# Last layer of a four-layer graph kernel: for the units on the diagonal, VectorE raises the distances and GpSimd weights the edges in three steps

## The reference, cut to what matters

```python
deg = jnp.maximum(adj.sum(axis=1, keepdims=True), 1e-08)
w = adj / deg
log_ij = _logmap(x[:, None, :], x[None, :, :], 1.0)      # for every pair i, j
agg = jnp.einsum('ij,ijc->ic', w, log_ij)
out = _expmap(zeros, agg @ weight + bias, 1.0)           # then residual and layer norm
```

## Time and profile before

| what | us |
|---|---|
| median of three executions | 1662.96 |
| lowest, highest | 1653.44, 1667.85 |
| the profiled execution | 1664.92 |
| its span, first to last instruction | 1662.80 |
| last layer, first raise (L1442) to end of the last weighting (L674) | 1157.51 to 1608.20 |

### The profile page before, as it was taken

The page is one execution under the profiler, slowest core; times in us unless marked ns, Lnnn a source line. Parts: engine busy times, 40 slices in busy tenths (PEclk is TensorE's granted clock), DMA queues, the critical chain, the costliest instruction groups (busy, mean ns, idle before and its releaser), DMA issues.

```text
span 1662.8 us, 20844 instructions
## 1 busy us (share of the span) xinstructions
PE 1508.1 (91%) x7990; PEld 633.8 (38%) x7990; DVE 1175.8 (71%) x1579; ACT 946.1 (57%) x918; POOL 306.3 (18%) x154
## 2 busy tenths in 40 slices
PE   5999999989999699999999999988788889889870
PEld 1433333333333444444444444433333333333330
DVE  4677755557888655755857847477888787887867
ACT  1243388854343423323334346667889898998954
POOL 1000000000000000000000004594445343444430
PEclk9999999999999699999999999999999999999995
DMA  9999779968999334443443422246344454544500
GB/s 343 411 412 413 291 285 409 409 275 354 413 412 369 120 148 156 156 185 116 152 152 150 155 102 64 76 133 197 109 134 166 155 179 135 173 133 146 164 14 26
DMA packets 118107, 348.95 MB, mean 210 GB/s; under 512 B 6325, under 2 KB 31225, under 8 KB 117753
## 3 DMA queue, kind: packets, MB, share of 16 engines
q1 hardware_dynamic: 106784, 329.27, 52.9%
q10 hardware_dynamic: 11224, 18.36, 3.0%
HBM read 329.78 MB, written 17.83 MB: 209 GB/s over the span
## 4 chain that ended last, share of the span: by engine, by line
PE 62%; issue 15%; POOL 11%; DVE 6%; DMA 3%; ACT 2%; SPq 0%; POOLq 0%; ACTq 0%; DVEq 0%
PE ps L777 19%; PE ps L904 13%; POOL ring L674 11%; PE ps L910 10%; PE ps L715 4%; PE ps L716 3%; DMA ring<-in_adjT 3%; PE ps L933 2%; PE ps L849 2%; PE ps L741 1%; PE ps L939 1%; PE ps L731 1%; PE ps L797 1%; PE ps L851 1%; PE ps L853 1%
## 5 line engine op out<-in xcount | busy, mean ns | idle before, releaser
L1184 ACT ACTIVATE work<-ps,code_bias 128x1024 uint8<-128x1024 f32 x128 | 135.8, 1111 | 247.0 <-PE ps L716 238.7
L904 PE MATMUL ps<-ring,X 128*64 128x512 f32 x512 | 264.1, 597 | 13.3 <-DVE ring L1943 13.3
L905 PE MATMUL ps<-work,X 128*64 128x512 f32 x512 | 264.1, 598 | 0.0
L635 POOL TENSOR_SCALAR work<-ring 128x1024 int16<-128x1024 uint8 x24 | 69.4, 2898 | 1025.0 <-DMA ring<-codes 978.5
L1315 ACT ACTIVATE work<-ring 128x2048 f32<-128x2048 f32 x64 | 122.2, 1911 | 217.1 <-PE ps L912 196.1
L674 POOL TENSOR_TENSOR ring<-ring,work 128x1024 f32<-128x1024 f32 x80 | 190.0, 2375 | 253.1 <-DVE work L2199 252.9
L910 PE MATMUL ps<-work 128*64 128x512 bf16 x768 | 208.7, 381 | 0.0
L912 PE MATMUL ps<-work 128*64 128x512 bf16 x768 | 208.7, 381 | 0.0
L1006 PE MATMUL ps<-work 128*128 128x512 f32 x320 | 165.6, 642 | 0.0
L777 PE MATMUL ps<-ring,work 128*64 128x512 f32 x704 | 161.0, 599 | 1.1 <-DMA ring<-in_adjT 1.1
L1940 DVE TENSOR_SCALAR work<-ring 128x2048 bf16<-128x2048 f32 x64 | 78.5, 1226 | 107.3 <-PE ps L912 107.1
(11 more groups left out here) (332 smaller groups left out, 2642.5 us busy)
## 6 DMA issues: line engine op xcount, KB each, us to landing
ring<-in_adjT SPq DMA_DIRECT2D x90, 2048.0 KB, 11.5
work<-in_adjT SPq DMA_DIRECT2D x26, 2048.0 KB, 15.4
ring<-in_adjT SPq DMA_DIRECT2D x48, 1024.0 KB, 8.1
codes<-work ACTq DMA_DIRECT2D x64, 256.0 KB, 6.1
ring<-codes SPq DMA_DIRECT2D x32, 512.0 KB, 3.6
ring<-in_adjT SPq DMA_DIRECT2D x32, 512.0 KB, 3.5
X<-in_x ACTq DMA_DIRECT2D x1, 1024.0 KB, 6.8
work<-in_xT SPq DMA_DIRECT2D x2, 512.0 KB, 23.2
```

The costliest lines, as they stand in the source:

```text
L904: nc.tensor.matmul(ps[0:F, h, :], rows, ring[:, r, k, cols], start=start, stop=stop)
L905: nc.tensor.matmul(ps[F:P, h, :], rows, negs[:, pair, i, cols], start=start, stop=stop)
L1184: nc.scalar.activation(codes[:, u, k:k + 2, :].rearrange("p k c -> p (k c)"), ps[:, bank:bank + 2, :].rearrange("p k c -> p (k c)"), ACT.Relu,
```

## The change

Own units only. Their raise moves from ScalarE to VectorE, straight ahead of `multiply` there (a `tensor_scalar` with add and max from PSUM into `u.log`, and a wait of VectorE on its own semaphore before `multiply`). Their angle product on VectorE goes. GpSimd takes it over: edges x inverse root as soon as that exists, then the angle clipped in place, then edges x angle. `wait_for_log` gives the raise of unit n the right releaser of the log buffer of unit n-3: the angle product of an off unit or the first GpSimd step of an own one. `g_made` now counts off units alone.

```diff
--- before.py
+++ after.py
@@ -271,6 +271,14 @@
         def off_at(n):
             u = unit_at(n)
             return u if u and u.off else None
+
+        def wait_for_log(eng, u):
+
+            w = unit_at(u.n - 3)
+            if w and w.off:
+                eng.wait_ge(g_made, w.offs + 1)
+            if w and not w.off:
+                eng.wait_ge(edges_scaled, w.place + 1)
 
         PAIRS = 2 * NS
         L2_TILES = [(Q, s) for part in ((0, 1, 2, 3), (4, 5), (6, 7)) for Q in (0, 1) for s in part]
@@ -390,7 +398,9 @@
         last_signs_copied = sem("last_signs_copied")
         rows_cleared = sem("rows_cleared")
         dist_ready = sem("dist_ready")
-        raised = sem("raised")
+        raised = [sem(f"raised_{e}") for e in ("dve", "act")]
+        edges_scaled = sem("edges_scaled")
+        angles_clipped = sem("angles_clipped")
         far_added = sem("far_added")
         prod_made = sem("prod_made")
         log_made = sem("log_made")
@@ -666,12 +676,19 @@
                 pool.wait_ge(last_signs_copied, 2 * h + 2)
 
             for u in units:
-                pool.wait_ge(g_made, u.n + 1)
                 if u.off:
+                    pool.wait_ge(g_made, u.offs + 1)
                     pool.wait_ge(edges_in[0][u.place // 2 % 2], (u.place // 4 + 1) * 16)
+                    nc.gpsimd.tensor_tensor(u.edges, u.edges, u.angle, ALU.mult).then_inc(weighted, 1)
                 else:
                     pool.wait_ge(edges_in[1][u.place % 2], (u.place // 2 + 1) * 16)
-                nc.gpsimd.tensor_tensor(u.edges, u.edges, u.angle, ALU.mult).then_inc(weighted, 1)
+                    pool.wait_ge(inv_made, u.n + 1)
+                    nc.gpsimd.tensor_tensor(u.edges, u.edges, u.log, ALU.mult).then_inc(edges_scaled, 1)
+                    pool.wait_ge(edges_scaled, u.place + 1)
+                    pool.wait_ge(angle_made, u.n + 1)
+                    nc.gpsimd.tensor_scalar(u.angle, u.angle, ANGLE_CLIP, None, ALU.min).then_inc(angles_clipped, 1)
+                    pool.wait_ge(angles_clipped, u.place + 1)
+                    nc.gpsimd.tensor_tensor(u.edges, u.edges, u.angle, ALU.mult).then_inc(weighted, 1)
                 if u.n == 2:
                     pool.wait_ge(weighted, u.n + 1)
                     copy_third_signs()
@@ -1038,7 +1055,7 @@
             def turn_g(u, h):
 
                 if h == 0:
-                    pe.wait_ge(g_made, u.n + 1)
+                    pe.wait_ge(g_made, u.offs + 1)
                 if u.offs or h:
                     pe.wait_ge(mirror_weighted, 2 * u.offs + h)
                 else:
@@ -1437,10 +1454,9 @@
             def raise_dist(u):
 
                 act.wait_ge(dist_ready, u.n + 1)
-                if u.n >= 3:
-                    act.wait_ge(g_made, u.n - 2)
+                wait_for_log(act, u)
                 nc.scalar.activation(u.log, ps[:, u.banks:u.banks + 2, :].rearrange("p h c -> p (h c)"),
-                                     ACT.Relu, bias=DIST_SCALE, scale=1.0).then_inc(raised, 1)
+                                     ACT.Relu, bias=DIST_SCALE, scale=1.0).then_inc(raised[1], 1)
 
             raise_dist(units[0])
             for n in range(LAST_PERIOD):
@@ -1462,7 +1478,7 @@
                     nc.scalar.activation(u.angle, u.log, ACT.Exp, scale=0.5).then_inc(root_made, 1)
                 if n == 0:
                     copy_nodes(2)
-                if unit_at(n + 1):
+                if off_at(n + 1):
                     raise_dist(units[n + 1])
                 if n == 5:
                     root2(2)
@@ -2108,7 +2124,14 @@
 
             def multiply(u):
 
-                dve.wait_ge(raised, u.n + 1)
+                if u.off:
+                    dve.wait_ge(raised[1], u.offs + 1)
+                else:
+                    dve.wait_ge(dist_ready, u.n + 1)
+                    wait_for_log(dve, u)
+                    V.tensor_scalar(u.log, ps[:, u.banks:u.banks + 2, :].rearrange("p h c -> p (h c)"), DIST_SCALE, 0.0,
+                                    ALU.add, ALU.max).then_inc(raised[0], 1)
+                    dve.wait_ge(raised[0], u.place + 1)
                 V.scalar_tensor_tensor(u.log, ps[:, u.banks:u.banks + 2, :].rearrange("p h c -> p (h c)"), 0.0, u.log,
                                        ALU.max, ALU.mult).then_inc(prod_made, 1)
 
@@ -2192,7 +2215,7 @@
                 if n - 1 in products_end[:-1]:
                     quad = products_end.index(n - 1)
                     add_mirror(quad, units[quad_ends[quad]])
-                v = unit_at(n - 1)
+                v = off_at(n - 1)
                 if v:
                     dve.wait_ge(angle_made, v.n + 1)
                     dve.wait_ge(inv_made, v.n + 1)
```

## The result

The changed kernel takes 1717.2 us (median of 4, 1707.9 to 1722.3) against 1660.2 for the kernel before: 1.033 times as long, 95% interval 1.029 to 1.037. The profiled execution took 1722.3 us against 1664.9, 57 us more. Nearly all of it, 55.6 us, lies between the first multiply and the end of the last weighting of the last layer: 449.6 us before (1158.57 to 1608.20), 505.3 after (1159.61 to 1664.86).

What follows compares the result with a forecast made beforehand. It took a closed loop through TensorE, ScalarE and VectorE, 4.90 us per unit, as the bound. 15 x 2.1 = 31.5, - 3 at the start, + 1.2 last five, + 6.5 end: 36 us, forecast 1700 us, range 1676 to 1724.

Steps and rivals of the forecast that it cites:

- the clock: Rival: TensorE idles about 3 us in one piece, its clock falls once every five units, 19 us more, 1720; chance 0.16.
- The loop and the raise behind the sum: Last layer: 4.90 us loop per unit; own units' raise on VectorE stands behind the sum, five units 27.4 against 26.2.
- place four covers it: Own unit at position four, counted from zero, of five: late distances cover the wait for the sum, only 0.2 us lost.
- Nothing for the missing angle product, nothing back from ScalarE: Own units: dropping VectorE's 1.14 us angle product gains nothing; ScalarE's two missing raises (2 x 0.9 us) return nearly nothing.
- The faster case: Rival: ScalarE sets the pace, so 32 raises x 0.92 = 29 us go, the end gives back 6.5: 1642; chance 0.09.
- GpSimd's clip: Own units' angle clip on GpSimd: 2.77 us, making three steps hold GpSimd for 7.7 us per own unit.
- the rival that hung on it: Rival, no collisions: with a clip of 1.5 us or less the third step ends early; 22 us, 1687; chance 0.20.
- The collision: VectorE's angle product, with two SBUF inputs, waits for GpSimd's current step: 0.85 us more for each five units.
- Start: First three groups of five units, VectorE fullest: the exchange of operations costs half, 3 us off the sum.
- Middle: Last layer's groups of five units after the first three: each + 2.1 us, some 28.3 instead of 26.2.
- The gather loses nothing: GpSimd's three steps end some 8.8 us after the inverse starts, the gather came 10.0 after: no loss, by about 1 us.
- End: Last two units, both own: GpSimd's six steps add 6.5 us, besides + 1.2 for the last five.

Runs made afterwards that it cites:

- no_clip: The changed kernel without GpSimd's clip of own units' angles, so two GpSimd steps instead of three; 1.017 times the kernel before.
- pool_only: The changed kernel with every raise back on ScalarE, leaving GpSimd's three steps and the missing angle product; 1.020 times the kernel before.
- raise_only: The kernel before with only own units' raise moved to VectorE, angle product and single GpSimd step as before; 1.014 times the kernel before.
- keep_clock10: The changed kernel with 10 small products of zeros on TensorE ahead of the push at place two, in 12 of 15 groups; 1.028 times the kernel before.
- The filling: Small products of zeros added to the changed kernel in TensorE's longest gap; with 10 of them, 1.028 and, repeated, 1.032 times the kernel before.

## Why the prediction was right or wrong

- **Direction and range.** Forecast slower, 1700 us, range 1676 to 1724; measured 1717. The forecast was + 36, the measured change + 57: the sum found two thirds of it. That the range holds 1717 it owes to the room that I left for the clock, a term that the sum hadn't.
- **The loop and the raise behind the sum.** Right to a tenth: sum, then raise 1.13 later, then multiply 1.24 later; alone it gives 27.5 for five, forecast 27.4. That place four covers it was right (0.15 to 0.3 us), and shown by raising only there.
- **Nothing for the missing angle product, nothing back from ScalarE.** Right: ScalarE has 23 us less to do and the end comes later. The faster case fell with the loop of 4.9 us, which every clean group keeps.
- **GpSimd's clip.** Taken as 2.77, measured 2.76 or 2.77 in 28 of the 32; the other four took 3.1, and each began while a VectorE operation with its inputs in SBUF still ran for 0.45 us or a little more. The Trainium skill (GPSIMD Engine Reference, "Engine selection") calls one-input work roughly line-rate, by its clock an estimated 0.85 us; this trace does not agree, and the rival that hung on it fell. With a shorter stay on GpSimd (no_clip) that rival's group of 27.5 does come.
- **The collision.** Right in mechanism and size: 28.3 us for five in clean groups, as forecast, products of 2.9 and 1.7 us that end 1.09 after GpSimd's step; 15 of the 48 took 1.8 us or more, the one in three that I had given as a sign. The Trainium skill (SBUF — State Buffer, "Who interferes with whom") has it that a VectorE instruction with two SBUF inputs contends with a GpSimd one that reads SBUF, for a pair of ports that one of them holds alone; the 2.81 us of pool_only agree.
- **Start.** This step failed: "there the exchange of one VectorE operation for another costs less, and I take half, 3 us off". It left 3.3 us for the first fifteen units; measured 9.6, of which 6.4 in units 5 to 9. Nothing came cheaper there: raise_only shows + 2.8 and pool_only + 5.3, together near the + 9.6, and the clock was 0.90 in 1180 to 1240 against 0.97. With the clock at 0.95 in these units instead of 0.90 (keep_clock10) they took 99.1 us instead of 101.2, so 2 us are shown to be the clock's; how the rest divides stays open.
- **Middle.** 12 groups x 2.1 = 25 us forecast, 39.7 measured. The groups without a fall fit. The term that was missing is seen at place three, which takes 4.9 without a fall: in nine of the twelve groups the distances behind the gap took longer than 1.98 us, up to 3.78, at a granted clock of 0.50 to 0.62 (1.00 in the two clean groups), and these nine add up to 16.0 us, more than the 14 to 15 that the sum lacked; other places gave a little back. It is the clock, which I had priced as a rival of its own (19 us over 13 groups) and left out of the sum. The price was low for a full fall (1.5, measured 2.2) and high in number (nine of twelve, four of them in part). The step that failed is thus the choice: my own schedule gave a gap of 3 us in every group, and I had one row of what such a gap does, and still gave it 0.16.
- **The gather loses nothing, "by about 1 us".** Nearly right. One group from unit 15 on, that of units 15 to 19, had 7.1 at place three without a fall, since GpSimd had two small steps of other work to do and the gather of unit 14 waited 2.88 us for it: 2.2 us.
- **End.** 1.2 + 6.5 = 7.7 forecast, 6.3 measured. pool_only alone has + 6.9 and raise_only + 1.2: nearly all of it is GpSimd's chain.

That the clock makes up the whole rest isn't shown. The filling took away 11.1 of the 16.0 us at place three; the other 4.9 lie in the three groups that had no filling. But it cost 3.9 in units 15 to 19 and let other places grow, so that the last layer as a whole got only 4 to 8 us shorter. How the falls that remain divide between the change and the small products stays open.

## What to carry to other kernels

Ask of a moved instruction not what it takes, but what stands ahead of it on its new engine at the moment its input is ready: the same raise cost 1.1 us at one place of the pattern and 0.15 at another. A step given to GpSimd must be over before VectorE's next instruction with two SBUF inputs, or that one waits for it. And when a worked schedule leaves TensorE a gap of 2.4 us in every round where it had one of 0.6, the lower clock belongs in the sum, not among the rivals.

## What the runs showed that I had not expected

Short gaps were followed by a fall too: in raise_only one of 1.63 us by distances of 3.68 us instead of 1.98 (1489.08), and another of the same 1.63 by none (1432.63, units 47 and 48). In the changed kernel gaps of 2.4 and 2.5 went without a fall in some groups (1612.62) and with one in others (1335.55). One second half of a mirror, 0.68 us long, moved ahead of one instruction, was worth 1.0% of the program by the times and 12.8 us (0.8%) in the last layer's trace, more than the 0.5% its plain schedule gave, since the three groups with the small products gained 1.6 to 2.5 us each. And the part of the program ahead of the last layer's first multiply, which does the same work in all these kernels, took from 1149.5 to 1163.1 us in the profiled executions: a difference of a few us between two kernels is better read from the layer that was changed than from the whole.
